# Two heads of a pair side by side on the partitions of a fused attention block

## The reference, cut to what matters

```python
q = (xn @ Wq).reshape(b, n, h, dh).transpose(0, 2, 1, 3)
kv = x @ Wkv
...
k = jnp.concatenate([nk, k], axis=2)
v = jnp.concatenate([nv, v], axis=2)
q = _l2norm(q) * q_scale
k = _l2norm(k) * k_scale
sim = jnp.einsum('bhid,bhjd->bhij', q, k) * SCALE
...
sim = sim + slopes * bias
...
sim = jnp.where(causal[None, None], -neg, sim)
attn = jax.nn.softmax(sim, axis=-1)
out = jnp.einsum('bhij,bhjd->bhid', attn, v)
```

## Time and profile before

| | us |
|---|---|
| runs, median of 3 | 3888.32 (3883.74 to 3893.57) |
| profiled execution, its own time | 3888.84 |
| its span, first to last instruction | 3886.7 |
| busy in the span: PE, DVE, ACT, POOL | 3410.9, 3246.1, 2830.7, 2006.9 |

### The profile page before, as it was taken

The page is one execution under the profiler, slowest core; times in us unless marked ns, Lnnn a source line. Parts: engine busy times, 40 slices in busy tenths (PEclk is TensorE's granted clock), DMA queues, the critical chain, the costliest instruction groups (busy, mean ns, idle before and its releaser), DMA issues.

```text
span 3886.7 us, 97861 instructions
## 1 busy us (share of the span) xinstructions
PE 3410.9 (88%) x35857; PEld 2291.0 (59%) x35857; DVE 3246.1 (84%) x8403; ACT 2830.7 (73%) x5453; POOL 2006.9 (52%) x2052
## 2 busy tenths in 40 slices
PE   1689989898998989889988998989989899898998
PEld 0356666565665656656665666656656566665665
DVE  6788888788887888888887888888888788887886
ACT  2477777677777778777787777777777677777776
POOL 2564455645556445554447445474454744556443
PEclk7789999999999999999999999989999899999999
DMA  3000000000010000100001001010000000000000
GB/s 129 21 15 2 21 21 31 20 2 23 18 37 15 2 23 26 34 10 2 29 23 39 2 4 34 23 31 2 15 26 29 23 2 23 18 34 12 2 2 23
DMA packets 41335, 82.39 MB, mean 21 GB/s; under 512 B 5792, under 2 KB 5792, under 8 KB 40352
## 3 DMA queue, kind: packets, MB, share of 16 engines
q1 hardware_dynamic: 36864, 67.13, 5.5%
q10 hardware_dynamic: 4000, 9.02, 0.6%
HBM read 59.36 MB, written 16.78 MB: 20 GB/s over the span
## 4 chain that ended last, share of the span: by engine, by line
PE 41%; DVE 24%; POOL 15%; issue 12%; ACT 7%; DMA 0%; ACTq 0%; POOLq 0%; DVEq 0%
DVE PS L780 5%; PE PS L969 5%; PE PS L970 5%; PE PS L971 5%; POOL RN L641 5%; PE PS L955 4%; DVE PL L850 4%; DVE Q2T L877 4%; PE PS L990 3%; PE PS L991 3%; PE PS L1032 2%; POOL QKB L634 2%; POOL STR L645 2%; DVE QKB L914 2%; ACT TOK L477 2%
## 5 line engine op out<-in xcount | busy, mean ns | idle before, releaser
L442 ACT ACTIVATE PR<-PS,BT,SC 128x512 f32<-128x512 f32 (+3 forms) x1536 | 1024.0, 667 | 360.0 <-PE PS L993 318.2
L780 DVE CUSTOM_DVE_ANT_0 PS<-PS,STR 128x512 f32<-128x512 f32 (+3 forms) x1536 | 834.4, 566 | 107.7 <-PE PS L955 97.7
L447 ACT ACTIVATE PH<-PR 128x512 f16<-128x512 f32 (+3 forms) x1536 | 804.0, 523 | 48.7
L850 DVE TENSOR_TENSOR PL<-PR,PH 128x512 f16<-128x512 f32 (+3 forms) x1152 | 692.5, 601 | 2.4 <-ACT PH L447 2.1
L641 POOL TENSOR_TENSOR RN<-SS,HALF 128x8 f32<-128x8 f32 x256 | 422.8, 1652 | 522.8 <-DVE SS L863 520.4
L969 PE MATMUL PS<-WH,XT 128*128 128x384 f16 x2048 | 671.3, 328 | 18.6 <-DVE QKB L801 18.6
L1022 PE MATMUL PS<-AR,PH 128*128 128x66 f16 x4608 | 612.7, 199 | 74.2 <-ACT PH L447 40.0
L970 PE MATMUL PS<-WL,XT 128*128 128x384 f16 x2048 | 669.7, 327 | 0.0
L971 PE MATMUL PS<-WH,XT 128*128 128x384 f16 x2048 | 669.6, 327 | 0.0
L593 POOL TENSOR_TENSOR PL<-PR,PH 128x512 f16<-128x512 f32 x384 | 449.1, 1169 | 423.2 <-ACT PH L447 416.5
L955 PE MATMUL PS<-AR 128*128 128x512 f16 (+3 forms) x1536 | 542.6, 353 | 137.6 <-DVE MX L780 91.4
(11 more groups left out here) (178 smaller groups left out, 7364.8 us busy)
## 6 DMA issues: line engine op xcount, KB each, us to landing
XW<-in_L_attn_x SPq DMA_DIRECT2D x128, 256.0 KB, 2.6
ACC<-in_L_attn_x SPq DMA_DIRECT2D x64, 256.0 KB, 2.6
out<-ACC SPq DMA_DIRECT2D x64, 256.0 KB, 2.0
AR<-in_L_attn_Wkv ACTq DMA_DIRECT2D x1, 4096.0 KB, 20.4
AR<-in_L_attn_Wq ACTq DMA_DIRECT2D x1, 2048.0 KB, 11.3
ACC<-in_L_attn_Wout ACTq DMA_DIRECT2D x1, 2048.0 KB, 25.1
LG<-in_L_ffn_ln_g ACTq DMA_DIRECT2D x1, 256.0 KB, 5.6
LB<-in_L_ffn_ln_b ACTq DMA_DIRECT2D x1, 256.0 KB, 5.8
```

What stands on the lines that cost most here:

```text
L442: e.activation(PR[:, n % 3, 0:wide], PS[:, n % 2, 0:wide], ACT.Exp, bias=BT[:, 2 * (u % NP) + h, kt - 4 * qc + 4:kt - 4 * qc + 5], scale=S ...
L447: e.activation(PH[:, n % 4, 0:wide], PR[:, n % 3, 0:wide], ACT.Copy).then_inc(s_ph, 1)
L780: e.tensor_tensor_reduce(out=r[:, 0:n], in0=r[:, 0:n], in1=ST[:, h, o:o + n], scale=1.0, scalar=LOW, op0=ALU.add, op1=ALU.max, accum_out=M ...
L850: e.tensor_tensor(PL[:, n % 3, 0:wide], PR[:, n % 3, 0:wide], PH[:, n % 4, 0:wide], ALU.subtract).then_inc(s_pl, 1)
```

## The change

Both heads of a pair now lie in one operand: head 0 on partitions 0 to 63, head 1 on 64 to 127. `KQ` holds four parts, `QH`, `QL`, `KH`, `KL`. A unit has 12 score steps and 12 piece pairs in place of 24 and 24, and every second slot has one of each; the slots of a unit stay 24.

- A piece is two matmuls of 64 rows, one for each head, in two banks of the ring. A score step is four such pairs into banks 0 and 1 (high-high, low-high, high-low, and a product `AL` by `CT` that holds alibi and shift), and the mask on diagonal tiles for both heads. The scores have one pair of banks, so the step waits for the exponential of the step before (before: of the one two steps back).
- One exponential, one fp16 copy and one low part for both heads (1024 columns at full width, now without a bias operand). All low parts are taken by DVE.
- The projection has 388 columns: 4 more are null scores, by weights that are worked out in the set-up; q's bias is added by one matmul (L1003) for each tile. It has one bank in place of two, and its tiles come every 3 slots in place of 2.
- The normalising product runs on POOL (L620, 512 columns, in place of 256). PE transposes fp32 (four for each group), and ACT and DVE make high and low parts behind the transpose, straight into `KQ`. Steps `HI`, `LO`, `Q2`, `NS`, the copies to `K2` and `Q2` and the thin null matmuls are gone. A transposed `CT` row block (L1102) takes the place of `Q2`.
- The null product is one matmul of 32 rows and 264 columns for each head and half.
- The set-up issues 48 transfers of null values in place of 12, and makes the null weights with two products of 4096 columns on POOL, each summed on DVE.

```diff
-STEPS = [(h, qc, kt) for qc in range(2) for h in range(2) for kt in range(4 * qc + 4)]
...
-W_SCORE = [SL + i for i in range(SL)]
-W_PLOW = [SL + i + 1 for i in range(SL)]
-W_VALUE = [SL + i + 3 for i in range(SL)]
...
+PIECES = [(qt, c) for qt in range(NT) for c in range(1 + qt // 4)]
+STEPS = [(qc, kt) for qc in range(2) for kt in range(4 * qc + 4)]
+NS = len(STEPS)
+W_PIECE = [16, 18, 20, 22, 24, 26, 28, 30, 32, 34, 36, 38]
+W_SCORE = [36 + 2 * i for i in range(NS)]
+W_PLOW = [36 + 2 * i + 1 for i in range(NS)]
+W_VALUE = [36 + 2 * i + 3 for i in range(NS)]
...
+W_SQ = [6 * g + 6 for g in range(4)]
+W_SS = [6 * g + 7 for g in range(4)]
+W_POW = [6 * g + 8 for g in range(4)]
+W_T1 = [6 * g + 9 for g in range(4)]
+W_TP = [6 * g + 10 for g in range(4)]
+W_HI = [6 * g + 11 for g in range(4)]
...
+W_SHIFT = [24, 39]
+W_CTP = [25, 40]
+W_CT = [26, 41]
...
+        SB, AV, PJ = PS[:, 0:2, :], PS[:, 2:4, 0:264], PS[:, 4, 0:WC]
...
-            for part in range(3):
-                for g in range(2):
-                    for n in range(2):
-                        row = part * 4 + g * 2 + n
-                        e.dma_start(HV[row:row + 1, g, :, 0:DH], nv[g:g + 1, :, 2 * n + 1, :]).then_inc(s_nv, 16)
+            for g in range(2):
+                for q in range(4):
+                    for part in range(3):
+                        for n in range(2):
+                            row = 32 * g + 8 * q + 2 * part + n
+                            e.dma_start(HV[row:row + 1, q, :, 0:DH], nv[g:g + 1, :, 2 * n + 1, :]).then_inc(s_nv, 16)
...
-                    w.wait_ge(s_st, n + 1)
-                    pl_done(w, n - 3)
-                    e.activation(PR[:, n % 3, 0:wide], PS[:, n % 2, 0:wide], ACT.Exp,
-                                 bias=BT[:, 2 * (u % NP) + h, kt - 4 * qc + 4:kt - 4 * qc + 5], scale=SIG).then_inc(s_p, 1)
+                    w.wait_ge(s_st, 2 * n + 2)
+                    w.wait_ge(s_pl, n - 1)
+                    e.activation(PR[:, n % 2, :, 0:wide], SB[:, :, 0:wide], ACT.Exp, scale=SIG).then_inc(s_p, 1)
                     w.wait_ge(s_p, n + 1)
-                    if n > 3:
-                        w.wait_ge(s_av, n - 3)
-                    e.activation(PH[:, n % 4, 0:wide], PR[:, n % 3, 0:wide], ACT.Copy).then_inc(s_ph, 1)
...
+                    e.activation(KQ[:, u % 2, QH, gs], rb("tp", u, g)[:, 0:256], ACT.Copy, scale=W2T[:, :]).then_inc(s_hi, 1)
+                    e.activation(KQ[:, u % 2, KH, gs], rb("tp", u, g)[:, 256:512], ACT.Copy, scale=KA).then_inc(s_hi, 1)
...
+                if n:
+                    w.wait_ge(s_wnf, 1)
+                e.tensor_tensor(WNT, WQS, KNB[:, n, :, :].rearrange("p (a h) d -> p a (h d)", a=1).to_broadcast([P, KC, 1024]),
+                                ALU.mult).then_inc(s_wnt, 1)
...
+                    e.tensor_tensor(
+                        QKB[:, i % 2, :, 0:256].rearrange("p t (j c) -> p t j c", c=64),
+                        QKB[:, i % 2, :, 0:256].rearrange("p t (j c) -> p t j c", c=64),
+                        RN[:, i % 2, :].rearrange("p (t j a) -> p t j a", t=2, a=1).to_broadcast([P, 2, 4, 64]),
+                        ALU.mult).then_inc(s_t1, 1)
...
+                    e.tensor_tensor(PL[:, n % 3, :, 0:wide], PR[:, n % 2, :, 0:wide], PH[:, n % 3, :, 0:wide],
+                                    ALU.subtract).then_inc(s_pl, 1)
...
+                    w.wait_ge(s_hi, 2 * i + 2)
+                    e.scalar_tensor_tensor(out=KQ[:, u % 2, QL, gs], in0=rb("tp", u, g)[:, 0:256], scalar=W2T[:, :],
+                                           in1=KQ[:, u % 2, QH, gs], op0=ALU.mult, op1=ALU.subtract).then_inc(s_lo, 1)
+                    e.scalar_tensor_tensor(out=KQ[:, u % 2, KL, gs], in0=rb("tp", u, g)[:, 256:512], scalar=KA,
+                                           in1=KQ[:, u % 2, KH, gs], op0=ALU.mult, op1=ALU.subtract).then_inc(s_lo, 1)
...
+                    e.matmul(PJ[:, 128:260], ONB[:, :], BQR[:, p, :], start=False, stop=False, skip_group_check=True)
...
+                    bank_free(w, "s", u, 2 * i)
+                    bank_free(w, "s", u, 2 * i + 1)
+                    w.wait_ge(s_hi, 2 * (4 * u + qt // 2) + 2)
+                    for h in range(2):
+                        hs = slice(64 * h, 64 * h + 64)
+                        e.matmul(rb("s", u, 2 * i + h)[:, 0:n], KQ[hs, u % 2, QH, P * qt:P * qt + P],
+                                 KQ[hs, u % 2, KH, 512 * c:512 * c + n], start=True, stop=True).then_inc(s_s, 1)
...
-                    if n > 1:
-                        w.wait_ge(s_p, n - 1)
-                    w.wait_ge(s_q2, 2 * u + qc + 1)
-                    w.wait_ge(s_k2, 4 * u + kt // 2 + 1)
-                    e.matmul(bank, KQ[:, u % 2, 2 + h, ks], KQ[:, u % 2, h, q0:q0 + wide], start=True, stop=False)
-                    ins = e.matmul(bank, K2[0:65, u % 2, h, ks], Q2[0:65, u % 2, h, q0:q0 + wide], start=False, stop=kt < 4 * qc)
...
+                    w.wait_ge(s_p, n)
+                    w.wait_ge(s_lo, 2 * (4 * u + max(2 * qc + 1, kt // 2)) + 2)
+                    w.wait_ge(s_ct, 2 * u + qc + 1)
+                    for a, c in ((KH, QH), (KL, QH), (KH, QL)):
+                        for h in range(2):
+                            hs = slice(64 * h, 64 * h + 64)
+                            e.matmul(SB[:, h, 0:wide], KQ[hs, u % 2, a, ks], KQ[hs, u % 2, c, qs], start=(a, c) == (KH, QH),
+                                     stop=False)
+                    for h in range(2):
+                        hs = slice(64 * h, 64 * h + 64)
+                        ins = e.matmul(SB[:, h, 0:wide], AL[hs, kt - 4 * qc + 4, :], CT[hs, u % 2, qs], start=False,
+                                       stop=kt < 4 * qc)
+                        if kt < 4 * qc:
+                            ins.then_inc(s_st, 1)
                     if kt >= 4 * qc:
-                        ins = e.matmul(bank[:, 0:P], TRI[:, :], IDB[:, :], start=False, stop=True)
-                    ins.then_inc(s_st, 1)
-                for u, i in due(s, W_PIECE[1]):
-                    piece(u, i)
+                        for h in range(2):
+                            e.matmul(SB[:, h, 0:P], TRI[:, :], IDB[:, :], start=False, stop=True).then_inc(s_st, 1)
...
+                            hs = slice(32 * h, 32 * h + 32)
+                            e.matmul(AV[:, h, :], PNT[hs, qc, :], VNT[hs, u % NP, :], start=False, stop=True,
+                                     skip_group_check=True).then_inc(s_o, 1)
...
-                        for q in range(4):
-                            ins = e.matmul(bank[:, 66 * q:66 * q + 66], PT[:, P * q:P * q + P], VN[:, 2 * (u % NP) + h, :],
-                                           start=False, stop=True, skip_group_check=True)
```

More of the change, by code:

```diff
@@ L76 @@
+W_HI = [6 * g + 11 for g in range(4)]
+W_ROWS = [22, 37]
+W_SHIFT = [24, 39]
+W_CTP = [25, 40]
+W_CT = [26, 41]
+W_NX = [27, 41]
+W_NL = [28, 42]
+W_NTP = [31, 45]
+W_NT = [32, 46]
 W_XA = [2 * t - 1 - 2 * SL for t in range(NT)]
 W_STAT = [2 * t + 1 - 2 * SL for t in range(NT)]
[L78 to L82, removed]
+W_XB = [3 * t - 1 - SL for t in range(NT)]
@@ L83 @@
+W_XF = [3 * t + 2 - SL for t in range(NT)]
+W_XH = [3 * t + 3 - SL for t in range(NT)]
+W_XL = [3 * t + 4 - SL for t in range(NT)]
+W_XTP = [3 * t + 8 - SL for t in range(NT)]
 W_SMALL = [18 + 2 * k - 2 * SL for k in range(5)]
 W_VSC = [29 - 2 * SL]
-SLOTS = range(-2, SL * NU + 64)
+SLOTS = range(-2, SL * NU + 80)
 def due(slot, when, units=NU, period=SL):
@@ L91, in due @@
     for i, off in enumerate(when):
-        if off is not None and (slot - off) % period == 0 and 0 <= (slot - off) // period < units:
+        if (slot - off) % period == 0 and 0 <= (slot - off) // period < units:
             out.append(((slot - off) // period, i))
@@ L99, in due_base @@
     out = [(0, t) for t in range(NT) if SL + 3 * t + off == slot]
-    return out + [(b, t) for b, t in due(slot, [SL + 16 + 3 * t + off for t in range(NT)], NB, BL) if b]
+    late = [(32 + 3 * t if t < 4 else 38 + 3 * t) + off for t in range(NT)]
+    return out + [(b, t) for b, t in due(slot, late, NB, BL) if b]
 def due_ln(slot, when):
@@ L124, in ring_order @@
     for s in SLOTS:
[L125 to L128 removed]
+        for u, i in due(s, W_PIECE):
+            take("s", u, 2 * i)
+            take("s", u, 2 * i + 1)
         for u, t in due_op(s):
@@ L730, in _ @@
             ln_xf(0, 1)
+            for n in range(2):
+                w.wait_ge(s_wnt, n + 1)
+                e.tensor_reduce(WNF[:, :, :, n], WNT.rearrange("p k (h d) -> p k h d", d=DH), AXX, ALU.add).then_inc(s_wnf, 1)
+            w.wait_ge(s_wnf, 2)
             w.wait_ge(s_ar, 1)
@@ new lines, in _ @@
+            for part in range(3):
+                dc(e.tensor_copy(BQT, BQX))
+                if part < 2:
+                    dc(e.tensor_tensor(BQX, BQX, BQT, ALU.subtract))
+                if part == 0:
```

(4 more changed lines are left out.)

833 lines of the change are left out of this document (396 added, 437 removed).

## The result

The changed kernel takes 4852.06 us (median of 4 runs, 4849.87 to 4856.18), the kernel before 3886.73 beside it: 1.2482 times as long, 95% interval 1.246 to 1.2503. The forecast of 3572 us and its range are missed by far, and on the other side.

What follows compares the result with a forecast made beforehand. The prediction took PE as the bound, with DVE close behind. Start at 185 us, 51 of filling and draining, 64 units of 52.1 and 2 beside the span gave 3572 us; the 8-in-10 range was 3390 to 3880.

Steps and rivals of the forecast that it cites:

- the lost time after: TensorE's idle time, record tails and slower clock in the changed kernel: 6.8 us a unit, between 4.0 and 9.5.
- new waits: Waits the new order adds: score loop 2.5 us against 4.3, projection bank 0.9 in 2.2, both hidden; others priced separately.
- the lost time does not shrink: Rival on TensorE's waits: tighter order keeps 9.5 us a unit lost, 3745 us, up to 3900; chance 0.22.
- Work on TensorE: TensorE's own steps in a unit, tile changes included: 45.3 us, 3.6 less than before.
- The first rival: Pieces and scores: a pair's two matmuls do not overlap, up to 9.9 us a unit more, 4206 us; chance 0.13.
- The switch of tiles: TensorE changing between 64-row and 128-row matmuls: about 0.2 us in and out together, 14 times, 2.8 us a unit.
- the full tail: Rival at TensorE's tiling changes: each drain costs 0.16 us, 1.7 us a unit more, 3680 us; chance 0.10.
- The other engines: Busy time a unit: DVE 42.4 us, ACT below 40, POOL near 30; none becomes the bound.
- The chain from k's copy to the transpose: Squares, sums, power, product and queues between k's copy and its transpose: fit five slots, 10.9 us, hidden with little to spare.
- The 1 us a unit at slot 24 for the high parts: Piece in slot 24 waits for group 2's high parts made in slot 23: about 1 us a unit, likeliest on PE.
- Ends: Program start and finish: set-up 70 us longer, first projection at 185 us, filling and draining 51 us.
- The sign I had named: PE idle for transposes L1091 or piece L1018 by more than 2 us a unit would show the forecast wrong.

Runs made afterwards that it cites:

- retimed kernel: Changed kernel with copies and halves earlier in ScalarE's and VectorE's lists, scores ahead of pieces on TensorE, and slots moved; 3552.06 us, 0.9131 times the kernel before.
- the fourth bank: Changed kernel with row sums and the second head's own null rows left out, the PSUM bank so freed added to the ring of three; 3879.25 us.
- fillers: Changed kernel plus 91 matmuls of 248 columns a unit into unused columns, ahead of transposes and pieces where TensorE waits longest; 4765.07 us.

## Why the prediction was wrong

- **The step that failed: "the lost time after", with the new waits it rested on.** I put it between 4.0 and 9.5 us a unit and took 6.8. It was 72.2 less 45.3, 26.9 us: 17.7 of waits, and 9.2 of tails, a slower clock and whatever else stretches TensorE's steps, where the forecast kept 4.0. Of the waits 14.3 (883 us) were for the ring's banks. The bounds were those of the kernel before, carried over to another order of work; nothing in the earlier trace rows could bound waits that this order makes.
- **What I left out.** I asked of each new wait whether its own loop fits the slots, as the score's 2.5 us against 4.3. I didn't ask of the ring's banks what stands ahead of the releasing copy in its engine's list, where the exponential had become twice as wide. With the instructions held equal, having half of that work ahead of ScalarE's copies is worth 362 us; moving ScalarE's copies past it gave 521, and both engines' copies 841.
- **The rival "the lost time does not shrink"** named the right place and the wrong size: 3900 at most, with a chance of 0.22. Its own sentence, that the order is tighter, was not followed into the ring.
- **Work on TensorE: right.** A retimed kernel with 2.9 us of waits a unit takes 51.7, so its steps come to 48.8. To compare with that is 49.3, my 45.3 and the 4.0 for tails and clock. The pairs run side by side: six matmuls of 512 columns take 0.65 us, from 2013.48 to 2014.13, three widths and not six, and on the same rows they cost 8.4 us a unit of the 9.9 that I priced. The first rival, which had the other side, falls.
- **The switch of tiles: right in size.** In the retimed kernel (timeline of TensorE) the first 64-row matmul starts 0.26 us after a projection, where the next projection would start 0.16 after it, and the 128-row mask 0.31 after 512 columns that take 0.22: 0.1 each way, as taken, not the full tail.

```profile
2000.36 0.33 PE L1004 MATMUL PS<-WL,XT 128*128 128x388 f16 x1
2000.52 0.33 PE L1005 MATMUL PS<-WH,XT 128*128 128x388 f16 x1
2000.78 0.82 PE L1023 MATMUL PS<-AR 64*128 64x512 f16 x6
2001.44 0.38 PE L1027 MATMUL PS<-AR,AL 64*128 64x512 f16 x2
2001.75 0.29 PE L1033 MATMUL PS<-IDB,TRI 128*128 128x128 bf16 x2
```

- **The other engines: right.** DVE 43.7 (42.4 forecast), ACT 33.1 (below 40), POOL 27.1 (near 30) a unit.
- **New waits.** The score pair's one bank pair: no score wait stands among TensorE's ten largest, as said. The projection's bank: hidden for TensorE, 31.6 us in all. The chain from k's copy to the transpose: hidden nearly everywhere, 18.4 us for POOL's product. The 1 us a unit at slot 24 for the high parts: the pieces that take a transpose's bank, mostly those of slots 18, 24 and 30, stood 351.4 us for L930, 5.7 a unit. With the fourth bank the wait for the high parts themselves shows, and it is 0.5 us a unit (waits of TensorE in that run, 250 to 3700 us):

```profile
PE PS L1018 <- ACT AR L458: 29.7, 54, 0.6
```

- **Ends: right.** The first projection stands at 190.84 us (185 forecast; timeline of TensorE, to compare with the earlier trace rows):

```profile
190.84 0.53 PE L1001 MATMUL PS<-WH,XT 128*128 128x388 f16 x1
```

Filling and draining take 4852.1 less 190.8 less 64 times 72.2, 40 us (51).

- **The sign I had named** was the right one: TensorE idle for L1091 by 5.5 us a unit and for L1018 by 6.7, where more than 2 was to make the forecast wrong.

The retimed kernel meets the forecast's number, 3552 against 3572, with the unit of 52 us that it was made for. That doesn't make the prediction right, which was for this order of work. Whether the kernel before would gain as much from new slots wasn't tried: by the forecast's count it loses 9.5 us a unit too.

## What to carry to other kernels

When an operation is merged into one twice as long, list what stands behind it in its engine's order, and who waits for that; the merged operation's own loop may fit while a small copy behind it holds a buffer that an in-order engine wants next. For each buffer of a ring, go from each user to the release before it, and look whether that release stands in the same slot, and behind what. A wait of another engine that is long, as ACT's 1025 us for the projection here, may only be the echo of the bound engine's lateness: give the suspected buffer to either side and see which one pays.

## What the runs showed of the hardware

Half-height matmuls of two heads ran side by side at one head's price, and a change between 64-row and 128-row tiles cost about 0.1 us, less than the 0.17 by which a projection's record (0.33) outlasts the step to the next (0.16). After an idle time of 2.47 us TensorE's granted clock stood at 0.50, with projections 0.32 us apart; in a stretch of work without a wait it stood at 1.00, with projections 0.16 apart. Keeping the clock up bought little here: with fillers in the waits the granted clock rose from 0.87 to 0.96, and the time fell by 87 us of 4852, the fillers' own time included.
